# Reordered GpSimd work in the last pair, four-matmul router logits, one PSUM bank per tile in the last group, one activation table load fewer

## What is computed

```
xn = layernorm(x)                                   # 32 x 112 x 256
q, k, v = xn @ Wq, ctx @ Wk, ctx @ Wv               # 16 heads of 64; ctx is 32 x 375 x 128
x = x + tanh(g_xattn) * (softmax(q k^T / 8) v @ Wo + bo)
h = layernorm(x)                                    # 3584 tokens
gates = softmax(h @ router_w)                       # 14 experts, the best two are kept and renormed
routed = sum over the two experts of silu(rms(h) * rw @ w1) @ w2 * weight
shared = sum over two shared experts of the same form
out = x + tanh(g_ffn) * (routed + shared)
```

## Time and profile before

| | us |
|---|---|
| median of 3 runs | 1454.03 (1454.0 to 1455.53) |
| the profiled execution, its own time | 1453.46 |
| its span, first to last instruction | 1451.9 |
| PE busy | 1433.0 (99%) |
| DVE, ACT, GpSimd busy | 1081.6, 935.3, 458.0 |
| share of the chain that ended last: PE, all others | 94%, 6% |
| mean granted TensorE clock | 0.998 of full speed |

### The profile page before, as it was taken

One profiled execution on the slowest core, in us unless ns is written; L12 is line 12 of the kernel. 1 busy time (PEld: TensorE's weight loads), 2 busy tenths in 40 slices (PEclk: granted clock), 3 DMA queues, 4 the chain that ended last, 5 costly groups with the idle time before them and its releaser, 6 DMA issues.

```text
span 1451.9 us, 29493 instructions
## 1 busy us (share of the span) xinstructions
PE 1433.0 (99%) x9774; PEld 1346.5 (93%) x9774; DVE 1081.6 (74%) x2614; ACT 935.3 (64%) x2398; POOL 458.0 (32%) x688
## 2 busy tenths in 40 slices
PE   7999999999999999999999999998999999999998
PEld 6999999999999999999999999998789988888888
DVE  4878888888888888888798888877587544444448
ACT  6777777777777777777777777776453445454552
POOL 4313142231323313143131422326100145555520
PEclk9999999999999999999999999999999999999999
DMA  4010312303112131212303112150022356562235
GB/s 126 7 52 18 116 75 55 103 24 117 75 50 82 50 109 50 84 75 57 109 16 118 75 50 95 36 194 31 28 102 116 131 179 236 212 236 92 77 123 222
DMA packets 55794, 138.02 MB, mean 95 GB/s; under 512 B 10512, under 2 KB 38176, under 8 KB 52064
## 3 DMA queue, kind: packets, MB, share of 16 engines
q1 hardware_dynamic: 49024, 118.01, 23.6%
q0 software_dynamic: 6624, 18.13, 4.0%
HBM read 86.69 MB, written 49.43 MB: 94 GB/s over the span
## 4 chain that ended last, share of the span: by engine, by line
PE 94%; DVE 2%; issue 1%; ACT 1%; POOL 1%; DMA 1%; SPq 0%; ACTq 0%; POOLq 0%
PE bank L589 18%; PE bank L590 18%; PE bank L591 18%; PE bank L650 9%; PE bank L1720 7%; PE bank L1047 6%; PE bank L1039 5%; PE bank L1743 4%; PE bank L1747 2%; PE bank L1731 2%; PE bank L1705 1%; PE bank L1223 1%; PE bank L605 1%; DMA under_wq<-in_Wq 0%; POOL keep_w_in L1149 0%
## 5 line engine op out<-in xcount | busy, mean ns | idle before, releaser
L765 ACT ACTIVATE prob<-bank,nmax 128x375 f32<-128x375 f32 x448 | 258.8, 578 | 183.1 <-DVE nmax L874 181.1
L857 DVE TENSOR_TENSOR pT_lo<-bank,pT_hi 125x384 fp32r<-125x384 f32 x448 | 245.8, 549 | 31.6 <-ACT pT_hi L776 30.1
L874 DVE TENSOR_REDUCE nmax<-bank 128x1 f32<-128x375 f32 x448 | 240.9, 538 | 24.6 <-PE bank L591 24.1
L650 PE MATMUL bank<-keep_ident,prob 128*125 128x128 f32 x1344 | 221.3, 273 | 0.0
L776 ACT CAST pT_hi<-bank 125x384 fp32r<-125x384 f32 x448 | 212.6, 475 | 1.7 <-PE bank L650 1.7
L650 PEld LDWEIGHTS bank<-keep_ident,prob 128*125 128x125 f32 x1344 | 201.9, 187 | 5.7
L589 PE MATMUL bank<-attend_wvo_hi,zT_hi 128*112 128x256 f32 x512 | 169.6, 331 | 0.1
L589 PE MATMUL bank<-attend_kvT_hi,qp_hi 128*128 128x376 f32 x448 | 151.3, 338 | 4.6 <-ACT prob L765 4.5
L589 PE MATMUL bank<-pT_hi,kv_hi 125*128 125x448 f32 x384 | 152.9, 398 | 2.8 <-DVE zT_lo L857 1.3
L590 PE MATMUL bank<-attend_kvT_hi,qp_lo 128*128 128x376 f32 x448 | 150.2, 335 | 0.0
L591 PE MATMUL bank<-attend_kvT_lo,qp_hi 128*128 128x376 f32 x448 | 149.5, 334 | 0.0
(11 more groups left out here) (238 smaller groups left out, 3715.5 us busy)
## 6 DMA issues: line engine op xcount, KB each, us to landing
w_split<-we_split SPq DMA_DIRECT2D x14, 2048.0 KB, 7.4
keep_weights<-w_split SPq DMA_DIRECT2D x14, 2048.0 KB
we_in<-in_w SPq DMA_DIRECT2D x28, 512.0 KB, 6.1
keep_y_all<-y_rows SPq DMA_DIRECT2D x14, 512.0 KB, 8.9
kv_in<-in_ctx SPq DMA_DIRECT2D x32, 187.5 KB
h_rows<-hrow SPq DMA_DIRECT2D x32, 112.4 KB, 2.6
keep_h_in<-h_rows SPq DMA_DIRECT2D x7, 514.0 KB, 9.6
x_in<-in_x SPq DMA_DIRECT2D x16, 224.0 KB, 3.0
```

Source lines behind the costliest of these rows:

```text
L650: last = nc.tensor.transpose(turn_bank_of(s)[0:MP, c * P:(c + 1) * P], prob[:, s % NB, c * MP:(c + 1) * MP], ident[:])
L765: nc.scalar.activation(prob[:, s % NB, :], score_bank(s)[:, 0:M], ACT.Exp, bias=nmax[:, s % NB:s % NB + 1], accum_out=psum_[:, s % NB:s % ...
L857: return nc.vector.tensor_tensor(dst, src, hi.bitcast(F32), ALU.subtract)
L874: nc.vector.tensor_reduce(nmax[:, s % NB:s % NB + 1], score_bank(s)[:, 0:M], AX, ALU.max, negate=True).then_inc(max_ready, 1)
```

## The change

Four independent edits.

1. GpSimd in the last pair: all waits of the weight work refer to later tiles; of the second expert only w1 is scaled ahead of `ln2_root(29)`; the bias of batch 31 and the scaling of the second w2 stand behind it.
2. Router logits: hi and lo of the router's weights stand side by side, so one matmul multiplies hT_hi by both (28 output rows), and one adds hT_lo times hi: four per group where there were six. The result has 28 rows, and the transposes back to tokens become products with a 28 x 14 matrix of two stacked identities (`sum_parts`), which also adds the two halves. DVE makes `sum_parts` once.
3. Last group: each of its four tiles has a bank of its own (4 to 7), TensorE waits for the four adds of group 5 before it writes them, signals each tile of the last item by itself, and the last stores are of 2, 1 and 1 tiles.
4. The second load of the table with ln and exp is dropped.

```diff
@@ gpsimd in attend, last pair
-            sb["scale_shared"](pool, 0, lambda: scaled(4), lambda: scaled(6))
+            sb["scale_shared"](pool, 0, lambda: scaled(6), lambda: scaled(8))
+            sb["scale_half"](pool, 1, lambda: scaled(10))
+            ln2_root(2 * p - 1)
             add_bias(p, 1)
-            sb["scale_shared"](pool, 1, lambda: scaled(8), lambda: scaled(10))
-            ln2_root(2 * p - 1)
+            sb["scale_rest"](pool, 1, lambda: scaled(14))
             pool.wait_ge(side_done, job_index(p, Q[7]) + 1)
-            sb["split_shared"](pool, 0, lambda: scaled(14), lambda: scaled(16), lambda: scaled(18))
-            sb["split_shared"](pool, 1, lambda: scaled(20), lambda: scaled(22), lambda: scaled(24))
+            sb["split_shared"](pool, 0, lambda: scaled(16), lambda: scaled(18), lambda: scaled(20))
+            sb["split_shared"](pool, 1, lambda: scaled(22), lambda: scaled(24), lambda: scaled(26))
             ln2_root(2 * p)
             ln2_root(2 * p + 1)
@@ scalar in attend
-            nc.scalar.preload_act_table_set("natural_log_exp_and_others")
             for p in range(PAIRS):
@@ front
-        rwp = {q: buf("rw_" + q, [P, 2, E], F32R) for q in ("hi", "lo")}
+        rw_split = buf("rw_split", [P, 2, 2, E], F32R)
+        rwp = {q: rw_split[:, :, i, :] for i, q in enumerate(("hi", "lo"))}
+        sum_parts = buf("sum_parts", [2 * E, E])
...
+        def scale_half(pool, e, wait_first):
+...
+        def scale_rest(pool, e, wait_second):
             wait_second()
             nc.gpsimd.tensor_scalar(w2_in[:, e], w2_in[:, e], sb["tanh_g"][:, 1:2], None, ALU.mult).then_inc(w_step, 1)
+        def scale_shared(pool, e, wait_first, wait_second):
+            scale_half(pool, e, wait_first)
+            scale_rest(pool, e, wait_second)
@@ logits(pe, g)
-            for n, (k, (w, h)) in enumerate((k, q) for k in range(2) for q in PRODUCTS):
-                last = nc.tensor.matmul(lt_bank(g)[0:E, :], rwp[w][:, k, :], hT_of(sb, h, g)[:, k, :],
-                                        start=n == 0, stop=n == 5)
+            for k in range(2):
+                nc.tensor.matmul(lt_bank(g)[0:2 * E, :], rw_split[:, k, :, :].rearrange("p q e -> p (q e)"),
+                                 hT_of(sb, "hi", g)[:, k, :], start=k == 0, stop=k == 1, skip_group_check=True)
+                last = nc.tensor.matmul(lt_bank(g)[0:E, :], rwp["hi"][:, k, :], hT_of(sb, "lo", g)[:, k, :],
+                                        start=False, stop=k == 1, skip_group_check=True)
@@ turn_logits(g)
+                if g == 0:
+                    pe.wait_ge(sum_ok, 1)
                 for t in range(4):
-                    last = nc.tensor.transpose(l_bank(g)[:, t * E:(t + 1) * E], logitT[:, b, t * P:(t + 1) * P],
-                                               sb["ident"][0:E, 0:E])
+                    last = nc.tensor.matmul(l_bank(g)[:, t * E:(t + 1) * E], logitT[:, b, t * P:(t + 1) * P],
+                                            sum_parts[:, :], start=True, stop=True)
@@ split_router(dve), ahead of the split
+            nc.vector.tensor_tensor(sum_parts[:], sb["ident"][0:2 * E, 0:E], sb["ident"][0:2 * E, E:2 * E], ALU.add
+                                    ).then_inc(sum_ok, 1)
@@ copy_logits(dve, g)
-            nc.vector.tensor_copy(logitT[:, g % 2, :], lt_bank(g)[0:E, :]).then_inc(lt_copied, 1)
+            nc.vector.tensor_copy(logitT[:, g % 2, :], lt_bank(g)[0:2 * E, :]).then_inc(lt_copied, 1)
@@ shared_after
+        def out_bank(g, t):
+            return O_BANK[t] if g == GROUPS - 1 else O_BANK[2 * (g % 2) + t // 2]
...
-            for t in (0, 2):
-                sp.wait_ge(acc_done, 4 * (g - BEFORE) + t + 2)
-                sp.dma_start(by_group(io["out"], g)[:, t:t + 2, :], acc[:, 4 * g + t:4 * g + t + 2, :]).then_inc(out_stored, 16)
+            for t, n in ((0, 2), (2, 1), (3, 1)):
+                sp.wait_ge(acc_done, 4 * (g - BEFORE) + t + n)
+                sp.dma_start(by_group(io["out"], g)[:, t:t + n, :], acc[:, 4 * g + t:4 * g + t + n, :]).then_inc(out_stored, 16)
...
+                alone = items[i][0] == GROUPS - 1
+                if alone and e == 0:
+                    pe.wait_ge(acc_done, 4)
                 for t in range(4):
-                    last = shared_output(nc, sb, hid, e, t, O_BANK[2 * (items[i][0] % 2) + t // 2])
-                    if t % 2:
+                    last = shared_output(nc, sb, hid, e, t, out_bank(items[i][0], t), alone)
+                    if t % 2 or i == len(items) - 1:
                         last.then_inc(o_done, 1)
...
-                    dve.wait_ge(o_done, 2 * i + t // 2 + 1)
+                    dve.wait_ge(o_done, 2 * i + (t if i == len(items) - 1 else t // 2) + 1)
```

More of the change, by code:

```diff
@@ L1041, in shared_hidden, with shared_output @@
     return last
-def shared_output(nc, sb, hid, e, t, bank):
+def shared_output(nc, sb, hid, e, t, bank, alone=False):
+    half = 0 if alone else t % 2
     for n, (j, (h, w)) in enumerate((j, q) for j in range(4) for q in PRODUCTS):
-        last = nc.tensor.matmul(bank[:, (t % 2) * D:(t % 2 + 1) * D], hid[h][:, e, j, t * P:(t + 1) * P],
-                                sb["w2s_" + w][:, e, j, :], start=e == 0 and t % 2 == 0 and n == 0,
-                                stop=e == SHARED - 1 and t % 2 == 1 and n == 11, skip_group_check=True)
+        last = nc.tensor.matmul(bank[:, half * D:(half + 1) * D], hid[h][:, e, j, t * P:(t + 1) * P],
+                                sb["w2s_" + w][:, e, j, :], start=e == 0 and half == 0 and n == 0,
+                                stop=e == SHARED - 1 and (alone or half == 1) and n == 11, skip_group_check=True)
     return last
@@ L1105, in front @@
         lt_done, lt_copied, l_turned, l_ready = sem("lt_done"), sem("lt_copied"), sem("l_turned"), sem("l_ready")
+        sum_ok = sem("sum_ok")
         code_made, gate, exp_done = sem("code_made"), sem("gate"), sem("exp_done")
@@ L1142, in load_front @@
                 load_h(sp, g)
-        def scale_shared(pool, e, wait_first, wait_second):
+        def scale_half(pool, e, wait_first):
             pool.wait_ge(rms_landed, 16 * SHARED)
@@ L1350, in copy_logits @@
                 dve.wait_ge(l_turned, g - 1)
-            nc.vector.tensor_copy(logitT[:, g % 2, :], lt_bank(g)[0:E, :]).then_inc(lt_copied, 1)
+            nc.vector.tensor_copy(logitT[:, g % 2, :], lt_bank(g)[0:2 * E, :]).then_inc(lt_copied, 1)
         sb.update(turn=turn, logits=logits, rows_hi=rows_hi, rows_lo=rows_lo, copy_logits=copy_logits,
                   split_router=split_router, load_front=load_front, load_front_w1=load_front_w1,
-                  scale_shared=scale_shared, split_shared=split_shared)
+                  scale_shared=scale_shared, scale_half=scale_half, scale_rest=scale_rest, split_shared=split_shared)
         def vector(dve):
@@ L1869, in sync @@
             g = GROUPS - 1
-            for t in (0, 2):
-                sp.wait_ge(acc_done, 4 * (g - BEFORE) + t + 2)
-                sp.dma_start(by_group(io["out"], g)[:, t:t + 2, :], acc[:, 4 * g + t:4 * g + t + 2, :]).then_inc(out_stored, 16)
-            sp.wait_ge(out_stored, 16 * (GROUPS + 1))
+            for t, n in ((0, 2), (2, 1), (3, 1)):
+                sp.wait_ge(acc_done, 4 * (g - BEFORE) + t + n)
+                sp.dma_start(by_group(io["out"], g)[:, t:t + n, :], acc[:, 4 * g + t:4 * g + t + n, :]).then_inc(out_stored, 16)
+            sp.wait_ge(out_stored, 16 * (GROUPS + 2))
         def gpsimd(pool):
@@ L1910, in accumulate @@
                 for t in range(4):
-                    dve.wait_ge(o_done, 2 * i + t // 2 + 1)
+                    dve.wait_ge(o_done, 2 * i + (t if i == len(items) - 1 else t // 2) + 1)
                     dve.wait_ge(y_added, 4 * TOPK * order.index(g) + 4 + t + 1)
-                    out = O_BANK[2 * (g % 2) + t // 2][:, (t % 2) * D:(t % 2 + 1) * D]
+                    half = 0 if g == GROUPS - 1 else t % 2
+                    out = out_bank(g, t)[:, half * D:(half + 1) * D]
                     nc.vector.tensor_tensor(acc[:, 4 * g + t, :], out, acc[:, 4 * g + t, :], ALU.add).then_inc(acc_done, 1)
@@ L1963, in lay_out @@
     put(slots + 4 * slot, slot,
-        [("logitT", [E, 2, 4 * P], F32), ("logit", [P, TILES, E], F32), ("gate_prob", [P, TILES, E], F32),
+        [("logitT", [2 * E, 2, 4 * P], F32), ("logit", [P, TILES, E], F32), ("gate_prob", [P, TILES, E], F32),
          ("tie", [P, TILES, E], F32), ("scan1", [P, TILES, E], F32), ("ones", [P, P], F32),
```

## The result

The changed kernel takes 1450.87 us (median of 9 runs, 1449.69 to 1452.37) against 1454.40 of the kernel before on the same chip (9 runs): ratio 0.9973, 95% interval 0.9965 to 0.9981. That is 2.8 to 5.1 us faster. The forecast was 8.8 us and 1445.2, with a range that ended at 1448.9: the sign was right, the size was not. The profiled execution is the longest of the nine, 1452.37 us with a span of 1450.5, 1.4 us under the span of before.

What follows compares the result with a forecast made beforehand. The prediction took TensorE, busy 99% of the span, as the bound. Terms -7.1 - 0.7 - 1.1 + 0.1 = -8.8 us gave 1445.2 from the median 1454.03; forecast 1443.5 to 1447 (66%), wider range 1442.6 to 1448.9.

Steps and rivals of the forecast that it cites:

- The stop of the last pair: Last pair: reordering GpSimd's work ends ACT's 5.58 us wait and TensorE's stop; -7.1 us, bounds 3.4 to 7.3 gained.
- the attention steps are drawn out by GpSimd's gapless work: Last pair, part of a 12% rival that some stop remains: gives back 3 to 4 of the 7.1 us, 1448.7.
- The table load: First exponential: without ACT's second table load it starts 0.84 us earlier; -0.7 us, bounds 0.4 and 1.3 gained.
- The logits: Router: 14 fewer matmuls -3.2, products with `sum_parts` +2.4, a free group -0.3; -1.1 us, bounds 0.2 lost to 2.4 gained.
- TensorE runs without a gap: Between the changed places: TensorE has no gap and no transfer sets its pace, so all 8.8 us pass to the end.
- the last rival: Last group, 3%: its wait grows and the kernel is slower; over about 3 us brings the low clock, 10 gives 1457.7.
- The last group: Kernel's end: wait for group 5's adds +0.8, one add less -0.35, smaller last transfer -0.4; +0.1 us, bounds -0.9 and +0.7.
- The sum: Whole kernel: four terms give -8.8 us, 1445.2; all bounds at worst -2.9, at best -11.9.
- rival of four weight loads: Router, 3%: each float32 product brings four weight loads, another 8 x 0.085 us per group, +4.8 us, 1450.0.

Runs made afterwards that it cites:

- e9: The kernel before without the second table load of ScalarE, nothing else changed: ratio 0.9995 (0.9986 to 1.0005).
- e4: The changed kernel measured again, with nothing altered: 1448.08 us (1447.01 to 1451.53) against 1455.14, ratio 0.9958.
- e7: The changed kernel with transposes of 28 rows in place of the float32 products, halves added by DVE: 1447.20 us against 1454.51, ratio 0.9949.
- e10: The kernel before with the reordered GpSimd work and the second w2 pass held back until step 16's normalisation is done: 1447.73 us against 1455.26, ratio 0.9951.
- e2: The kernel before with only the router's logits changed, four matmuls per group and the summing product: 1457.20 us against 1455.14, ratio 1.0011.
- e6: The changed kernel with the products of group 5 moved behind the first six matmuls of the shared expert: 1449.82 us, ratio 0.9967 to the kernel before.
- e11: The kernel before with e10's order, one table load, e7's transposes but halves added once, last-group bank per tile with late waits: 1445.11 us against 1455.26, ratio 0.9936.

## Why the prediction was wrong

- **The stop of the last pair: the mechanism was right, and the size holds where the moved pass does not meet a normalisation.** ACT's wait went, the clock stayed up, no new wait came in front of batch 30. Where the normalisation isn't drawn out, the term is -7.06 for -7.1 forecast; where it is, -5.40 (both against A of the trace before). I costed the moved pass of w2 at nothing, with slack on GpSimd as the cover, and looked only at who waits for its result. I did not ask what DVE does while the pass runs, though the trace before shows 28 normalisations held until 0.2 us behind a GpSimd pass. The rival "the attention steps are drawn out by GpSimd's gapless work" had it, inside a mechanism with a price of 3 to 4; it cost 1.6.
- **The table load: right.** -0.75 for -0.7 at 65 us; that it reaches the end is not shown by e9's time.
- **The logits: the step that failed.** The cut matmuls gave what they should (0.23 us each, 0.46 per group). The products cost 0.99 us per group and not 0.68: I took 0.085 per record, from the transposes, with 0.1025 as the upper bound, and 0.124 lay above both. With 0.99 the forecast's own sum would have been +1.1 in place of -1.1; B without the fall shows +0.68, in part because the sixteen records in a row took 1.88 (e4) and all of the 0.43 wait went, not 0.3 of it. The nearest row was chosen by its column count; e7 shows that a transpose of the same 28 rows still takes 0.09, so neither rows nor columns but the float32 product is what costs.
- **What the sum lacked altogether:** the clock. "TensorE runs without a gap" was my reason why everything passes to the end, and in B it was without a gap. Its clock fell all the same, in two of the changed kernel's three traces, for 3.2 us each (B 413.57 and 413.60 to 410.42). I had met the low clock in the earlier trace rows, and took a stop to be its only cause. How long a stop must be for it ("more than about 3 us" in the last rival) no run shows: 3.39 us brought it, 1.73 in the kernel after did not.
- **The last group: near in size** (+0.25 for +0.1, within its bounds). The wait is 0.71 for 0.7. The tail behind the last matmul shrank by 0.7, within what I gave.
- **The sum, with what was measured:** -7.1 - 0.75 + 0.7 + 0.25 = -6.9 with neither trouble, which is the 1447 to 1448 us of the best executions, and -5.4 - 0.75 + 3.85 + 0.25 = -2.05 with both, which is the 1452.3 us of the worst. The measured median, 3.5 us under before, lies between them.

On the pages used: the SBUF — State Buffer page of the Trainium skill ("SBUF: two separate sides") says that DVE and GpSimd share a port pair as an exclusive lock: whichever starts first, a GpSimd operation or one of DVE in a two-port mode or with two SBUF inputs, has it for the whole instruction, and the other fully blocks. No run here shows in which mode the normalisation runs. The traces agree in all 28 cases beside the routed experts' weights and in five of six at step 16 (2.03 to 2.05 us), but not in e4, where the same normalisation ran inside the pass in 0.42. The FP8 and Floating Point Precision page of the Trainium skill ("TensorE Precision Notes") gives four passes for true FP32; the trace shows two records per product and 0.25 us for it (0.99 / 4), three times a transpose's 0.085. My rival of four weight loads would have made 0.34.

## What to carry to other kernels

When work is moved on one engine, look not only at who waits for its result but at what the neighbouring engine does meanwhile: a GpSimd pass of 2.9 us over memory may hold a 0.4 us DVE operation until 0.2 us behind its end, and the trace before may hold cases to read the price from. Put such a pass right behind the operation, with a wait if need be (e10: 1.6 us for nothing but other numbers in six waits).

A float32 product is no cheap way to turn or to add a few columns: it costs three transposes, and behind a stretch with many of them TensorE's clock fell with no gap to warn of it. Read the granted clock in every stretch that gets new short matmuls, over several executions.

## What the runs showed of the hardware that I had not expected

- TensorE's granted clock fell to 0.50 while it was busy in every 4 us stretch, behind 13 us of which the 14-column float32 products took 6 (1025.13 to 1038.28 in the kernel after). It lasted 3.4 us (e2) to 6.8 us (after), reckoned from the stretches above, came in some executions of one kernel and not in others on the same chip, and never showed in a trace of a kernel with transposes there. What decides it in one execution is open: e6 shows only that sixteen records in a row are not needed.
- A DVE normalisation that starts 0.7 to 1.0 us into a GpSimd pass over the routed experts' weights ends 0.21 us behind that pass, in every one of 28 cases per trace. Beside the passes over a shared expert's w2 (2.85 us) it is not so regular. Started 1.02 us into the second one it took 2.05 us in five traces and 0.42 in e4. Beside the first one it took 0.66 to 1.10 us when it started 0.2 to 0.7 us into it, and so ended 1.5 us before the pass did (eleven traces); started 0.97 to 1.17 us into it, it took 0.42 (e7, e10, e11). What decides that is open.
- Three stores (256, 128 and 128 KB) issued behind each other on one queue start 0.37 and 0.65 us apart in e11, and the last one's end comes 3.1 us after its start, against 2.6 in the kernel after, where it is issued by itself. So a finer last store seems to help only where the store before it is out of the way.
